# A two-layer graph kernel: the second layer one group later, P turned through DRAM, P summed before K V

## The reference, cut to what matters

```
h   = relu(layernorm(x))
z_l = h W_lang^T ;  z_g = h W_grav^T ;  v = h W_V^T
A_l = relu(cosine similarity of the rows of z_l), diagonal set to 0
A_g = exp(-|z_g[n] - z_g[m]|^2 / (2 sigma^2)),    diagonal set to 0
K   = w_l * row_normalized(A_l * adj) + (1 - w_l) * row_normalized(A_g * adj)
x   = x + (K v) W_O^T                     # layer 0
h2  = relu(layernorm(x))
x   = x + adj2^T h2 + bias                # layer 1, adj2 = adj * adj
```

## Time and profile before

| what | value |
|---|---|
| median of 3 runs | 1266.11 us (1265.71 to 1266.63) |
| profiled execution, its own time | 1266.65 us |
| span of its profile | 1264.8 us |
| PE busy | 1241.4 us (98%) |
| DVE / ACT / POOL busy | 84% / 55% / 46% |
| granted TensorE clock, mean | 0.994 |

### The profile page before, as it was taken

The page is one execution under the profiler, slowest core; times in us unless marked ns, Lnnn a source line. Parts: engine busy times, 40 slices in busy tenths (PEclk is TensorE's granted clock), DMA queues, the critical chain, the costliest instruction groups (busy, mean ns, idle before and its releaser), DMA issues.

```text
span 1264.8 us, 22572 instructions
## 1 busy us (share of the span) xinstructions
PE 1241.4 (98%) x6324; PEld 1039.9 (82%) x6324; DVE 1058.7 (84%) x1826; ACT 694.6 (55%) x1324; POOL 575.5 (46%) x964
## 2 busy tenths in 40 slices
PE   7999999999999999999999999999999999999996
PEld 7888888888888888888888888888888888888884
DVE  5688888898888898888898888898888898888777
ACT  6346655456655546655546655545655545664543
POOL 1124554434554434555444555444555343455433
PEclk9999999999999999999999999999999999999997
DMA  6233333443333444242444242444242334243201
GB/s 243 34 76 87 96 76 73 100 108 93 89 84 65 100 108 99 84 97 53 100 107 104 79 107 47 100 103 106 79 106 58 91 100 108 81 102 72 45 34 66
DMA packets 308894, 112.55 MB, mean 89 GB/s; under 512 B 269840, under 2 KB 269968, under 8 KB 308880
## 3 DMA queue, kind: packets, MB, share of 16 engines
q1 hardware_dynamic: 177360, 95.78, 27.6%
q10 hardware_dynamic: 131520, 16.60, 8.0%
HBM read 46.20 MB, written 33.62 MB: 63 GB/s over the span
## 4 chain that ended last, share of the span: by engine, by line
PE 92%; DVE 5%; issue 2%; ACT 1%; DMA 0%; DVEq 0%; ACTq 0%
PE ring L868 73%; PE p_ps L868 15%; PE p_ps L941 2%; PE kt_ps L881 1%; PE ring L958 1%; DVE x_out L689 1%; DVE y_lo L558 1%; PE p_ps L967 0%; DVE deg L603 0%; DMA x_ring<-in_L_gnn_W_lang 0%; DVE h L573 0%; DVE chain L587 0%; ACT v_hi L442 0%; DVE K L617 0%; ACT h L379 0%
## 5 line engine op out<-in xcount | busy, mean ns | idle before, releaser
L301 POOL TENSOR_TENSOR x_out<-x_ring,bias_sb 128x512 f32<-128x512 f32 x128 | 162.7, 1293 | 498.9 <-DVE bn L638 498.9
L406 ACT ACTIVATE y_hi<-ring 128x512 fp32r<-128x512 f32 x256 | 148.4, 593 | 201.8 <-PE ring L868 199.0
L868 PE MATMUL ring<-hT_hi,Lw_hi 128*128 128x512 f32 x640 | 256.4, 401 | 2.1 <-DVE hT_lo L577 1.3
L868 PE MATMUL ring<-hT_hi,Lw_lo 128*128 128x512 f32 x640 | 250.1, 391 | 0.0
L868 PE MATMUL ring<-hT_lo,Lw_hi 128*128 128x512 f32 x640 | 249.8, 390 | 0.0
L558 DVE TENSOR_TENSOR v_lo<-ring,v_hi 128x512 fp32r<-128x512 f32 x128 | 88.4, 692 | 137.2 <-ACT v_hi L442 137.2
L868 PE MATMUL ring<-MT_hi,hT_hi 128*128 128x512 f32 x512 | 202.6, 396 | 0.0
L868 PE MATMUL ring<-MT_lo,hT_hi 128*128 128x512 f32 x512 | 199.6, 390 | 0.0
L868 PE MATMUL ring<-MT_hi,hT_lo 128*128 128x512 f32 x512 | 199.6, 390 | 0.0
L308 POOL TENSOR_TENSOR h_lo<-h2f,h_hi 128x512 fp32r<-128x512 f32 x124 | 158.0, 1295 | 85.1 <-ACT h_hi L476 85.1
L558 DVE TENSOR_TENSOR y_lo<-ring,y_hi 128x512 fp32r<-128x512 f32 x256 | 168.8, 679 | 26.4 <-ACT y_hi L406 26.4
(11 more groups left out here) (160 smaller groups left out, 2539.6 us busy)
## 6 DMA issues: line engine op xcount, KB each, us to landing
x_ring<-in_x SPq DMA_DIRECT2D x32, 1024.0 KB, 5.5
out<-x_out SPq DMA_DIRECT2D x128, 256.0 KB, 2.2
h_turned<-h SPq DMA_DIRECT2D x248, 64.0 KB, 2.1
h_turned<-h ACTq DMA_DIRECT2D x248, 64.0 KB, 2.1
rn_cols<-rn_dram SPq DMA_DIRECT2D x31, 256.0 KB, 3.8
x_ring<-in_L_gnn_W_lang SPq DMA_DIRECT2D x4, 256.0 KB, 5.2
h2f<-in_L_gnn_W_grav SPq DMA_DIRECT2D x1, 1024.0 KB, 8.9
chain<-in_L_gnn_W_O SPq DMA_DIRECT2D x1, 1024.0 KB, 12.8
```

Source lines behind the costliest of these rows:

```text
L301: pool.tensor_tensor(x_out[:, b], x_rows(g, b), bias_sb[:, :], ALU.add).then_inc(x2b_ready, 1)
L406: act.activation(y[0][:, a, :, l], bank(n).rearrange("p (b m) -> p b m", b=GB), ACT.Copy)\
L868: mm = pe.matmul(out, lhsT, rhs, start=(k == 0), stop=(k == len(terms) - 1))
```

## The change

- *PE.* The P phase comes directly behind the y phase, and runs over the four feature chunks `a` outside and the four batches inside, so its first products need only the first `y_lo`. The transposes of K stand behind the second chunk. K V of group i-1 follows the P phase. Layer 1 in iteration i is that of group i-2. The 8 transposes of P are gone, but for the last group.
- *P turned through DRAM.* DVE transposes the 32x32 blocks of each side of P (`turn_p`, into the place of `diag`), SP stores the 256 KB to DRAM (`store_p`) and reads them back with four DMAs of 64 KB for each side (`fetch_p`), into the place of `h`. DVE adds P and its transpose at the third y block of the next iteration (`sum_s`), side by side.
- *Mask.* POOL multiplies the inverse norms with the mask (`mask_norms`), and `similarities` is gone.
- *Turning h.* All 16 DMAs are issued by SP. The second half of `turn_blocks` comes behind the last y block.
- *x.* Five slots. The bias and layer 1 are added in the slot of the group; `x_out` is gone. x of group i+2 is loaded when the outputs of i-3 are stored.
- *h2.* `h2_full` of group i-1 is made at the end of iteration i, `h2_copy` and `h2_lo` of it behind the y blocks of iteration i+1.
- *End.* The last iterations are written out: the layer 1 of group 30 stands between K V and layer 1 of group 31.

```diff
@@ SP @@
             def turn_h(g):
                 sp.wait_ge(blocks_ready, GB * g)
-                for i in range(NQ // 2):
+                for i in range(NQ):
...
+            def store_p(g, l):
+                sp.wait_ge(p_blocks, 2 * g + l + 1)
+                sp.dma_start(p_dram[l], P_blocks[:, l].rearrange("p j b q -> p j (b q)")).then_inc(p_stored[l], 16)
+
+            def fetch_p(g, l):
+                sp.wait_ge(p_stored[l], 16 * g + 16)
+                for j in range(NQ):
+                    sp.dma_start(P_turned[j * Q:(j + 1) * Q, l], p_dram[l][:, j].rearrange("(i r) e -> r i e", r=Q))\
+                      .then_inc(p_turned[l], 16)
...
-            def iteration(i, load=True, after=True):
-                if after:
-                    turn_h(i + 1)
-                if after:
-                    spread_norms(i)
-                store_out(i - 1, first_use(i) + PER - GB)
+            def iteration(i, load=True, lag=True):
                 if load:
-                    sp.wait_ge(x_loaded, 16 * i + 48)
-                    load_x(i + 3)
+
+                    sp.wait_ge(out_stored, 16 * GB * (i - 2))
+                    load_x(i + 2)
+                turn_h(i + 1)
+                spread_norms_turn_p(i)
+                if lag:
+                    store_out(i - 2, first_use(i) + PER - GB)
...
@@ POOL @@
+                if lag:
+                    for b in range(GB):
+                        h2_lo(i - 2, b)
+                    for b in range(GB):
+                        add_bias(i - 2, b)
+                row_norms(i)
                 if before:
-                    for b in range(GB // 2):
-                        add_bias(i - 1, b)
                     norm2(i - 1)
...
+                if after:
+                    mask_norms(i)
...
             iteration(NG - 1, after=False)
+            for b in range(GB):
+                h2_lo(NG - 2, b)
...
@@ DVE @@
+                if after:
+                    turn_blocks(i + 1, 2)
+                    turn_blocks(i + 1, 3)
+                    if x_next:
+                        x_stats(i + 2, 0, GB)
+                if not after:
+                    last_chain(i, n, use, hi)
+                    return
                 if before:
-                    residual(i - 1, n, first_use(i) + n, i + 2 if stats and after else None)
+                    kt_lo(i - 1)
+                    add(i - 1, 0, n)
+                    add(i - 1, 1, n + 1)
+                squared_norms(i)
+                if before:
+                    add(i - 1, 2, n + 2)
+                    add(i - 1, 3, n + 3)
...
                     turned_lo(i + 1, b)
-                    if b == (2 if before else GB - 1):
-                        sum_s(i)
-                if before:
+                    if before and b < GB // 2:
+                        stats(i - 1, 2 * b)
+                        stats(i - 1, 2 * b + 1)
+                    if b == 1:
+                        turn_p(i, 0)
+                        turn_p(i, 1)
+                if lag:
                     for b in range(GB):
-                        output(i - 1, b, n + b)
-                similarities(i)
-                mask_l(i)
+                        output(i - 2, b, n + b)
...
             g = NG - 1
-            residual(g, 0, first_use(NG), last=True)
+            last_residual(g, first_use(NG))
+            for b in range(GB):
+                output_bias(g - 1, b, GB + b)
             h2_lo(g, 0)
...
@@ PE @@
+                wait_for(pe, p_copied, 2 * i)
+                for a in range(C):
+                    pe.wait_ge(drained, use + 2 * a + 2)
+                    for b in range(GB):
+                        terms = passes([w[:, a, b] for w in hT], [w[:, a, b].rearrange("p l m -> p (l m)") for w in y])
...
+                    if before and a == 1:
+                        transposes_K(i - 1)
...
-                        layer1(i - 1, b, n + b, use + n + b)
+                        layer1(i - 2, b, n + b, use + n + b)
```

More of the change, by code:

```diff
@@ L72, in gnn_pair @@
         KT = [sb(f"KT_{s}", [P, GB, P], F32R) for s in ("hi", "lo")]
-        x_out = sb("x_out", [P, GB, D])
         h2f = sb("h2f", [P, GB, D])
@@ L115, in gnn_pair @@
         woT_parts = [w[:, :, :] for w in h2]
+        p_dram = [nc.dram_tensor(f"p_dram_{l}", [P, NQ, GB * Q], F32).ap() for l in range(2)]
         rn_dram = nc.dram_tensor("rn_dram", [P, GB], F32).ap()
@@ L165, in gnn_pair @@
         blocks_ready, turned = sem("blocks_ready"), sem("turned")
+        p_blocks = sem("p_blocks")
+        p_stored, p_turned = [[sem(f"p_{what}_{l}") for l in range(2)] for what in ("stored", "turned")]
         ht_hi, ht_lo = sem("ht_hi"), sem("ht_lo")
@@ L338, in _ @@
             pool.wait_ge(consts_loaded, 16 * 4)
-            iteration(0, before=False)
-            iteration(1)
+            iteration(0, before=False, lag=False)
+            iteration(1, lag=False)
             with pool.Fori(2, NG - 1) as i:
@@ L397, in turned_hi, with iteration @@
                 act.activation(hT_columns(0, b), h_columns(b), ACT.Copy).then_inc(ht_hi, 1)
-            def iteration(i, before=True, after=True):
+            def iteration(i, before=True, lag=True, after=True):
                 n = 0
@@ L411, in iteration @@
                             factor_hi(C + 2 * n - 1)
-                        if after and 3 <= n < 5:
-                            normalize(i + 1, (n - 3) * GB // 2)
-                        if before and n == 4:
-                            w_g_K_g(i - 1)
-                        if before and n == G_USES - 1:
-                            kt_copy(i - 1)
-                if after:
-                    turn_h(i + 1)
+                        if before and n == 3:
+                            exponentials(i - 1)
+                        if after and n == 5:
+                            normalize(i + 1, 0)
+                        if before and n == 6:
+                            w_g_K_g(i - 1)
+                        if after and n == 7:
+                            normalize(i + 1, GB // 2)
+                if lag:
+                    for b in range(GB):
+                        h2_copy(i - 2, b)
+                if before:
+                    kt_copy(i - 1)
+                    act.wait_ge(s_ready, 2 * i)
+                for half in range(2):
+                    act.wait_ge(p_done, GB * i + 2 * half + 2)
+                    act.activation(P_sb[:, 2 * half:2 * half + 2], p_ps[:, 2 * half:2 * half + 2], ACT.Copy)\
+                       .then_inc(p_copied, 1)
+                if not after:
+                    shift(i)
                 for c in range(C):
@@ L425, in iteration @@
                 if before:
-                    act.wait_ge(s_ready, i)
-                    act.wait_ge(diag_ready, 2 * i)
-                for half in range(2):
-                    act.wait_ge(p_done, GB * i + 2 * half + 2)
-                    act.activation(P_sb[:, 2 * half:2 * half + 2], p_ps[:, 2 * half:2 * half + 2], ACT.Copy)\
-                       .then_inc(p_copied, 1)
-                if not after:
-                    shift(i)
-                if before:
-                    h2_full(i - 1, 0)
-                    h2_full(i - 1, 1)
                     act.wait_ge(kv_done, GB * i)
@@ L937, in iteration @@
                     n += 1
-                    if b == (GB - 1 if not before else 2 if after else 0):
+                    if b == 0 and not after:
                         pe.wait_ge(p_shifted, i + 1)
@@ L942, in iteration @@
                         mm.then_inc(pt_done, 1)
-                        if not after:
-                            transposes_rn(i)
-                if before:
+                        transposes_rn(i)
+                if lag:
                     for b in range(GB):
@@ L992, in _ @@
             for b in range(GB):
-                layer1(g, b, b, use + GB + b, last=True)
+                layer1(g - 1, b, b, use + GB + b)
+            for b in range(GB):
+                layer1(g, b, b, use + 2 * GB + b, last=True)
 _INS = ["x", "adj", "L0_gnn_W_lang", "L0_gnn_W_grav", "L0_gnn_W_V", "L0_gnn_W_O",
```

266 lines of the change are left out of this document (139 added, 127 removed).

## The result

The changed kernel takes 1282.6 us (median of 4 runs, 1281.8 to 1283.5), the kernel before 1266.1: a ratio of 1.013, 95% interval 1.011 to 1.015. It is slower by 16.5 us. 1271 was predicted, with a range from 1243 to 1292.

A forecast was written before the change was run, and what follows sets the result against it. PE, 98% busy, was taken to bound the kernel before, and h's late turn the changed one. 1264.8 + 1.5 - 0.9 - 0.6 + 4.4 = 1269.2, with 1.85 outside the span 1271 us; range 1243 to 1292.

The forecast's parts named there:

- The decisive step: Turn of h on SP's queue: it lands late, making the period 37.8 us instead of PE's 36.6.
- Blocks, issue, landing: Turn of h, from T, the first y matmul: blocks T+16.6, 16 DMAs spaced 0.65, landed T+28.5, hT_hi 2.2 late.
- The period: Loop iteration: 29.15 + 7.9 + 0.73 = 37.8 us, +0.05 against before, 1.5 us over 29 iterations.
- the turn is hidden: Rival: one queue issues faster than 0.5, the turn lands by T+26.3, PE sets 36.6: 1236 us, chance 0.16.
- DVE alone behind the landing: From the first hT_lo, DVE runs 13 operations up to layer 1's first output, together 7.9 us.
- P through DRAM: Store and eight reads land P at T'+3.4, T' the next y phase; DVE reaches the sum at T'+4.9.
- DVE beside POOL: Rival: POOL's h_lo and bias hold up DVE's squares; two waits of 0.6 cost nothing, two of 1.29 give 1286; chance 0.15.
- A gap of 1 us before the y phase: Predicted sign on PE in every iteration: one gap of 1 us before the y phase, ended by DVE.
- Iteration 0: First iteration: the product of the weights between P and v hides the turn, -0.9 us.
- Iterations 1 and 2: Iteration 1 has no layer 1, so its period is 37.1, -0.6 us; iteration 2 as the loop, +0.05.
- The end: Last iterations: DVE adds 5.5, factors about 0.7, 1.8 given back by ACT and POOL: +4.4 us, from +1 to +7.
- The loop: The 28 periods behind iteration 2: +0.05 us each, +1.4 us.

The follow-up runs named there:

- e1_split: Changed kernel with ACT issuing 4 of the 16 DMAs that turn h and SP the other 12: 1234.2 us, ratio 0.975.
- e3_early: Changed kernel with the second two 32x32 transposes of h ahead of the last y_lo instead of behind it: 1262.8 us, ratio 0.997.
- e5_before_one: Kernel before the change, with all 16 DMAs that turn h issued by SP and none by ACT: 1265.6 us, ratio 1.000.
- e2_stats: Changed kernel with the first two of four statistics on DVE moved ahead of the first hT_lo: 1278.4 us, ratio 1.010.
- e8_stats_shift: Changed kernel with two statistics ahead of the first hT_lo on DVE and four shift activations ahead of the first hT_hi on ACT: 1246.4 us, ratio 0.985.
- e11_small_bias: Changed kernel with POOL's four bias additions an iteration on 8 columns in place of 512: 1280.1 us, ratio 1.011.
- e4_warm: Changed kernel with 20 matmuls whose result nobody reads put into PE's gap at the end of iteration 1: 1280.7 us, ratio 1.011.
- e12_last_block: e1_split with the last block of hT made ahead of v_hi and v_lo of the last batch in iterations 0 and 1: 1232.1 us, ratio 0.973.

## Why the prediction was right, and where not

The decisive step was right, in mechanism and in size: the time at which the turn lands sets the period. The size of the whole change was not: 4.4 us of span were forecast and 16.9 measured. The time lies in the range because the loop, with its 29 periods, was sized well, while the terms outside it came out 10 us too low together. That those errors were small against the range is no merit of the working.

- **Blocks, issue, landing.** Predicted T+16.6, spacing 0.65, first `hT_hi` late by 2.2, `hT_lo` at T+29.15. Measured T+16.5, 0.67, 2.50 and T+29.4. Three runs bear out that this sets the period: fewer issues in the queue (e1_split), earlier blocks (e3_early, one for one), and the same queue with time to spare (e5_before_one).
- **The period.** 37.8 predicted, 37.88 measured. The sign and the small size of the difference in the loop (+0.14 a period) are a near cancellation: 1.41 less for PE alone and 1.55 more waiting. The whole of the rival "the turn is hidden" was there to be had: e1_split is that case, 1234 where the rival said 1236. That they lie so close is in part luck: its period of 36.6 was 0.27 too long, some 7 us, and the terms outside the loop were too low by some 5.
- **DVE alone behind the landing.** The count of 13 operations gave the right 7.8 us, but the step was incomplete. ACT's queue of shift and `v_hi` is as long to within 0.2 us. For the forecast it made no difference; for an attempt to mend the kernel it made all of it (e2_stats against e8_stats_shift).
- **P through DRAM.** Predicted to land at T'+3.4, and the sum at T'+4.9 without a wait. Eight reads in 3.64 us from 644.00 on put the last one at about 647.2, and the page of the kernel after has the landing (count, KB, median us), which answers to the earlier trace rows:

```profile
h<-p_dram SPq DMA_DIRECT2D x248, 64.0 KB, 1.9
```

  So P has landed at T'+3.5, and the sum stands at T'+5.0 with no wait. Right, with 0.455 a read instead of 0.4.
- **DVE beside POOL.** The operations were stretched, by 0.32 and 0.38 where the rival had 0.6 each, and it cost nothing in the loop, as it also said (e11_small_bias). The transposes of h, with one input, were not: two of them take 1.29 beside POOL's `h_lo`, as they did before.
- **"A gap of 1 us before the y phase".** Wrong in form (the size is 1.35): the loss is spread over three joints, each ended by DVE.

The span lay 12.5 us above my sum. Besides 0.4 at the start, these terms were off:

- **Iteration 0** (-0.9 predicted, +1.6 measured). I had taken the whole 0.87 of P's transposes as won. But they filled part of a chain that is exposed at that place: before, PE waits 1.25 behind them, and after, 2.13. 0.87 + 1.25 = 2.12, so nothing was won. And v now waits 1.41 for `MT_lo`, since nothing stands between the products of the weights and v.
- **Iterations 1 and 2** (-0.6 predicted, +3.8 measured, of which e4_warm gives about 2 to the clock). A period of 37.1 in iteration 1, with less work for PE, holds a gap, but I worked out neither its length, 4.46, nor its price at the clock; the trace of before has no gap of that length behind the setup, and so no row with this price. Iteration 1 itself took 38.1: its 16 issues took 11.48 us instead of 10.4, and `hT_lo` came at T+30.2 instead of T+29.15.
- **The end** (+4.4 predicted, +7.4 measured, 0.4 outside the bounds of +1 to +7). Four times 0.7 + 0.65 is 5.4 and not 5.5, which changes little. The first `h_lo` came 7.8 later, not 6.2: the wait for h2 is 1.05, and the small factors beside POOL's `h_lo` take 1.24 instead of 0.16. The 1.8 that I had given back for ACT and POOL having run ahead was 0.4.
- **The loop** (+1.4 predicted, +3.7 measured for the 28 periods behind iteration 2): 0.08 us a period.

What stays open: what the landing itself would be with other queues (POOL's) was not tried, nor why PE waits longer for `v_lo` in iteration 2 than in the loop (0.73, and 1.03 in e4_warm, against 0.39).

## What to carry to other kernels

When an edit puts several small DMAs into one queue, count them: here each takes its queue 0.67 us, and the last one's landing is what the next stage sees. The same queue cost nothing 4 us earlier in the period and 1.55 us a period later on. Behind a late instruction every engine that waits has a queue of its own; shortening one of two equal ones brings 0.15, both 1.2. And work that is taken from an engine is worth only what doesn't lie over another chain's wait: look at what the removed instructions filled.

## What the runs showed of the hardware that I had not expected

- After a gap of 4.46 us PE was granted 0.50 of its clock (1.2 of 2.4 GHz) for 5.8 us. After one of 2.16 us (e1_split) it ran 0.9 us at full clock and then 3.2 us at 0.50. After 1.70 us (e12_last_block) and after 2.13 us at the end of iteration 0 it stayed at 1.00. So the length of the gap alone does not tell what the clock will do.
- VectorE and GpSimd slow each other: squares on DVE 1.03 instead of 0.68, POOL's additions 1.52 instead of the 1.29 of the earlier trace rows, an operation on 2 columns 1.24 instead of 0.16, an addition 1.76 instead of 0.69. A VectorE operation on 512 columns that begins second ends 0.55 us behind the GpSimd operation that was running, the one on 2 columns 0.02.
- 16 DMAs of 64 KB in pieces of 128 bytes take 0.67 us each on one queue, the 8 reads of P 0.455 each, at the same 64 KB and a quarter of the pieces; both land about 2 us after their issue.
